# Softmax attention with fp32 queries and keys, fp32 scores in two row halves, and a new share of the split between VectorE and GpSimd

## The reference

```python
q = shape(hidden_states @ w_q)            # 16 heads of 64
k = shape(hidden_states @ w_k)
v = shape(hidden_states @ w_v)
scores = jnp.einsum('bhqd,bhkd->bhqk', q, k)
scores = scores + position_bias           # by head and distance
attn = jax.nn.softmax(scores.astype(jnp.float32), axis=-1).astype(scores.dtype)
ctx = jnp.einsum('bhqk,bhkd->bhqd', attn, v)
ctx = jnp.transpose(ctx, (0, 2, 1, 3)).reshape(B, S, INNER)
return ctx @ w_o
```

## Time and profile before

| | us |
|---|---|
| median of 3 runs | 2856.32 |
| lowest, highest | 2848.78, 2875.38 |
| span of the profiled execution | 2683.3 |
| softmax attention in it: first scores | 1426.6 |
| VectorE, ScalarE busy over the whole span | 2185.8, 1708.2 |
| TensorE, GpSimd busy over the whole span | 2000.1, 1788.5 |

### The profile page before, as it was taken

How to read it: one execution, slowest core, us unless ns; L and a number is a source line. 1 busy time by engine, 2 the same in 40 slices (tenths; PEclk the granted TensorE clock), 3 DMA queues, 4 the chain that set the end, 5 groups by cost and what they waited for, 6 DMA issues and landing times. The chain is left out here.

```text
span 2683.3 us, 62873 instructions
## 1 busy us (share of the span) xinstructions
PE 2000.1 (75%) x15627; PEld 1459.9 (54%) x15627; DVE 2185.8 (81%) x8149; ACT 1708.2 (64%) x4680; POOL 1788.5 (67%) x2414
## 2 busy tenths in 40 slices
PE   2329997485336999128887999999999999995887
PEld 2219887364226988115563555555555555553565
DVE  5427999686434999588999999999999999997897
ACT  3215554453224555145557999999999999995564
POOL 5765777102774777435645888888888888885555
PEclk9999999797558999559998999999999999998999
DMA  5134443402124444430003765666566656663000
GB/s 182 53 81 121 130 129 106 133 8 102 53 72 109 129 127 129 147 109 1 0 0 79 135 138 134 138 138 140 131 140 139 140 134 137 138 137 80 16 20 28
DMA packets 703411, 272.39 MB, mean 102 GB/s; under 512 B 560020, under 2 KB 688852, under 8 KB 702468
## 3 DMA queue, kind: packets, MB, share of 16 engines
q1 hardware_dynamic: 680628, 229.75, 35.0%
q0 software_dynamic: 17408, 35.82, 4.2%
q10 hardware_dynamic: 5200, 4.84, 0.6%
HBM read 59.31 MB, written 44.24 MB: 39 GB/s over the span
## 5 line engine op out<-in xcount | busy, mean ns | idle before, releaser
L2219 ACT ACTIVATE p_prob<-p_neg,p_neg_max 128x256 f32<-128x256 f32 x1024 | 509.0, 502 | 6.0 <-DVE p_neg_max L2111 5.8
L1044 POOL DMA_INDIRECT results_by_token<-p_e_result,p_e_slot x288 | 283.8, 985 | 156.9 <-DVE p_e_result L987 80.4
L2111 DVE CUSTOM_DVE_ANT_0 p_neg<-p_s_ps,top_bias 128x256 f32<-128x256 f32 x1024 | 380.5, 406 | 0.0
L2313 POOL TENSOR_TENSOR p_parts<-p_prob,p_parts 128x512 f16<-128x512 f32 x320 | 368.3, 1159 | 0.0
L2306 POOL TENSOR_SCALAR p_prob<-p_prob,p_inverse 128x256 f32<-128x256 f32 x640 | 328.8, 526 | 35.3 <-DVE p_inverse L2117 35.2
L730 POOL DMA_INDIRECT rows_by_expert<-p_r_z,p_r_target x256 | 247.5, 967 | 125.6 <-issue 105.3
L2346 PE MATMUL p_o_ps<-p_probT,p_val 128*128 128x256 f16 x1024 | 282.5, 276 | 62.0 <-DMA p_probT<-p_parts 61.6
L881 PE MATMUL p_e_o_ps<-p_w,p_e_hT 128*128 x2304 | 281.3, 276 | 0.2
L2347 PE MATMUL p_o_ps<-p_probT,p_val 128*128 128x256 f16 x1024 | 279.2, 273 | 0.0
L2348 PE MATMUL p_o_ps<-p_probT,p_val 128*128 128x256 f16 x1024 | 279.2, 273 | 0.0
L881 PEld LDWEIGHTS p_e_o_ps<-p_w,p_e_hT 128*128 128x128 f32 x2304 | 268.4, 192 | 3.5 <-issue 1.8
(11 more groups left out here) (282 smaller groups left out, 5609.2 us busy)
## 6 DMA issues: line engine op xcount, KB each, us to landing
p_e_z<-rows_by_expert SPq DMA_DIRECT2D x144, 129.0 KB
p_e_affine<-p_affine SPq DMA_DIRECT2D x144, 128.0 KB, 2.0
p_got<-results_by_token SPq DMA_DIRECT2D x64, 256.0 KB, 2.9
p_e_b<-p_b SPq DMA_DIRECT2D x144, 64.0 KB
p_probT<-p_parts SPq DMA_TRANSPOSE x512, 2.8
results_by_token<-p_e_result,p_e_slot POOLq DMA_INDIRECT x288
p_r_w<-in_w SPq DMA_DIRECT2D x2, 2048.0 KB, 10.1
p_w<-in_w SPq DMA_DIRECT2D x2, 2048.0 KB, 12.5
```

What stands on the lines that cost most here:

```text
L1044: pool.indirect_dma_start(dram_results, bass.IndirectOffsetOnAxis(ap=slot[q][:, t:t + 1], axis=0), result[q % 2][:, t, :], None).then_inc( ...
L2111: ins = v.tensor_tensor_reduce(neg[k % NEGS][:, t, :], s_ps[k % SCORES][:, t, :], bias[:, t, h, :], -1.0 / SCORE_SCALE, HUGE, ALU.add, ALU ...
L2219: ins = act.activation(prob[k % PROBS][:, t, :], neg[k % NEGS][:, t, :], ACT.Exp, bias=neg_max[k % NEGS][:, t:t + 1], scale=-1.0, accum_ou ...
L2313: pool.tensor_tensor(parts[k % PROBS][:, LOW, :, :], prob[k % PROBS][:], parts[k % PROBS][:, HIGH, :, :], ALU.subtract)\
```

## The change

1. Queries and keys are kept once, in fp32, instead of in two fp16 parts. ScalarE copies the bank and frees it; VectorE's low parts of queries and keys are gone. The scale of scores and bias becomes one.
2. Scores are fp32 matmuls: for each of two row tiles one in each row half, so 4 for a pair of units in the code in place of 12.
3. `SPLIT_BY` goes from three units of eight by VectorE (0, 2, 4) to five (0, 1, 3, 5, 6).
4. The projection slots of a quad alternate: query and key of the first pair, a pair of value tiles, query and key of the second pair, the other pair of value tiles. Value tiles still get two parts.
5. Semaphore counts follow. At the end, the last units' extra steps are only done where GpSimd splits the unit.

```diff
-FIRST_BANK = ((Q, 0), (Q, 1), (V, 0), (V, 2))
-SECOND_BANK = ((K, 0), (K, 1), (V, 1), (V, 3))
+FIRST_BANK = ((Q, 0), (V, 0), (Q, 1), (V, 2))
+SECOND_BANK = ((K, 0), (V, 1), (K, 1), (V, 3))
+PAIR_SLOTS = (0, 2)
+VALUE_SLOTS = (1, 3)
...
-SPLIT_BY = (BY_VECTOR, BY_POOL, BY_VECTOR, BY_POOL, BY_VECTOR, BY_POOL, BY_POOL, BY_POOL)
+SPLIT_BY = (BY_VECTOR, BY_VECTOR, BY_POOL, BY_VECTOR, BY_POOL, BY_VECTOR, BY_VECTOR, BY_POOL)
...
-        qkT = [m.sb(f"qkT{b}", [P, 2, 2, QUAD_PAIRS, GN], F16) for b in range(2)]
+        qkT = [m.sb(f"qkT{b}", [P, 2, QUAD_PAIRS, GN]) for b in range(2)]
...
-                    if has_slot(g, j // 2, ahead):
-                        (keep_low_second if j % 2 else keep_low_first)(*projection(i, g, j // 2))
+                    if j // 2 in VALUE_SLOTS:
+                        (keep_low_second if j % 2 else keep_low_first)(i, g, j // 2)
...
-            for n in range(QUAD_PAIRS):
-                keep_low_first(0, 0, n)
-                keep_low_second(0, 0, n)
             for k in range(3):
                 biased_max(0, k)
...
-            def take_high_first(i, g, n):
+            def take_first(i, g, n):
                 act.wait_ge(act_done, first_number(i, g, n))
-                high, scale = kept(g, HIGH, FIRST_BANK[n])
-                act.activation(high, act_ps[:], ACT.Copy, scale=scale).then_inc(high_ready, 1)
...
+                of, at = FIRST_BANK[n]
+                if of == V:
+                    act.activation(value(g, HIGH, at), act_ps[:], ACT.Copy, scale=VALUE_SCALE / (Z_SCALE * B_SCALE)).then_inc(high_ready, 1)
+                else:
+                    act.activation(qkT[g % 2][:, of, at, :], act_ps[:], ACT.Copy, scale=1.0 / (Z_SCALE * A_SCALE)).then_inc(act_taken, 1)
...
                 for k in range(1, GROUP_UNITS, 2):
-                    normalise(i, k)
+                    (high_part if split_by(k) == BY_VECTOR else normalise)(i, k)
...
-                passes = ((HIGH, HIGH), (HIGH, LOW), (LOW, HIGH))
                 for t in range(SEQ_TILES):
                     rows = slice(b * SEQ + t * P, b * SEQ + (t + 1) * P)
-                    for n, (q_part, k_part) in enumerate(passes):
-                        for h in range(2):
-                            half = slice(h * D_HEAD, (h + 1) * D_HEAD)
-                            ins = pe.matmul(s_ps[(k + h) % SCORES][:, t, :], qkT[g % 2][half, q_part, Q, pair, rows],
-                                            qkT[g % 2][half, k_part, K, pair, toks], start=n == 0, stop=n + 1 == len(passes))
...
+                    for h in range(2):
+                        half = slice(h * D_HEAD, (h + 1) * D_HEAD)
+                        ins = pe.matmul(s_ps[(k + h) % SCORES][:, t, :], qkT[g % 2][half, Q, pair, rows], qkT[g % 2][half, K, pair, toks],
+                                        start=True, stop=True)
...
-                    pe.wait_ge(act_taken, first_number(i, g, 2 + b))
-                    pe.wait_ge(v_taken, second_number(i, g, 2 + b))
+                    pe.wait_ge(act_taken, first_number(i, g, VALUE_SLOTS[b]))
+                    pe.wait_ge(v_taken, second_number(i, g, VALUE_SLOTS[b]))
```

More of the change, by code:

```diff
@@ L1736 @@
 A_SCALE = 2.0 ** 4
-QK_SCALE = 2.0 ** 5
 B_SCALE = 2.0 ** 4
@@ L1964, in g_use, with unmade @@
[L1964 to L1970, removed]
         def first_group(i):
             return isinstance(i, int) and i == 0
-        def second_use(i, g, n):
-            return i * (QUADS * GT) + (QUAD_PAIRS + g * GT + n - unmade(i, g))
+        def unmade(i, g, n):
+            return sum(slot <= n for slot in PAIR_SLOTS) if last_group(i) and g == QUADS - 1 else 0
@@ L2126, in keep_low_second @@
             def keep_low_second(i, g, n):
[L2127 to L2129 removed]
+                v.wait_ge(v_high, second_high_number(i, g, n))
+                tile = SECOND_BANK[n][1]
+                v.scalar_tensor_tensor(value(g, LOW, tile), v_ps[:], VALUE_SCALE / (Z_SCALE * B_SCALE), value(g, HIGH, tile),
+                                       ALU.mult, ALU.subtract).then_inc(v_taken, 1)
             def keep_low_z(i):
[L2132 removed]
+                v.wait_ge(high_ready, high_z_number(i))
                 v.scalar_tensor_tensor(zT[:, 1, :], act_ps[:], Z_SCALE, zT[:, 0, :], ALU.mult, ALU.subtract)\
@@ L2136, in keep_low_first @@
             def keep_low_first(i, g, n):
-                v.wait_ge(high_ready, first_number(i, g, n))
-                (high, scale), (low, _) = (kept(g, part, FIRST_BANK[n]) for part in (HIGH, LOW))
-                v.scalar_tensor_tensor(low, act_ps[:], scale, high, ALU.mult, ALU.subtract).then_inc(act_taken, 1)
+                v.wait_ge(high_ready, high_number(i, g, n))
+                tile = FIRST_BANK[n][1]
+                v.scalar_tensor_tensor(value(g, LOW, tile), act_ps[:], VALUE_SCALE / (Z_SCALE * B_SCALE), value(g, HIGH, tile),
+                                       ALU.mult, ALU.subtract).then_inc(act_taken, 1)
             def add_output(i, b):
@@ L2271, in _ @@
             take_high_z(0)
-            for n in range(QUAD_PAIRS):
-                take_high_first(0, 0, n)
-                take_high_second(0, 0, n)
+            for n in PAIR_SLOTS:
+                take_first(0, 0, n)
+                take_second(0, 0, n)
             exponent(0, 0)
@@ L2282, in _ @@
             for k in range(GROUP_UNITS - 2, GROUP_UNITS):
-                high_part(last, k)
+                if split_by(k) == BY_POOL:
+                    high_part(last, k)
             for b in range(GROUP_SEQS):
@@ L2444, in _ @@
                 ins.then_inc(b_done, 1)
-            turn_z(0, 0)
+            turn_z(0)
             pe.wait_ge(qk_low, 2)
-            for n in range(QUAD_PAIRS):
+            for n in PAIR_SLOTS:
                 project_first(0, 0, n)
```

91 lines of the change are left out of this document (52 added, 39 removed).

## The result

The changed kernel takes 2880.96 us (median of 9 runs, 2872.01 to 2893.74) against 2852.56 us for the kernel before on the same chip (9 runs): 1.0103 times as long, interval 1.0076 to 1.0129, +28.4 us. (A ratio is taken over all runs, not from the two medians.) The prediction was about 2884 us, +28. A second comparison gave 1.0101 (1.0068 to 1.0133), +32.4 us.

A forecast was written before the change was run, and what follows sets the result against it. VectorE, with ScalarE nearly full, was taken to set the pace: 65.3 - 63.4 = 1.9 us a group, times 16 groups, less 2 at the ends, +28; 2856.3 + 28 = about 2884 us, range 2815 to 2920.

The forecast's parts named there:

- the walk: Step-by-step timing of one round of eight units on VectorE and GpSimd; four rounds plus 1.9 us gave 64.7 to 66.7 us.
- the lower half: VectorE's period taken as 65.3 of 64.7 to 66.7 us, since a VectorE held up by TensorE meets fewer subtractions.
- slots 1, 2 and 6: VectorE's unit steps in a round of eight where GpSimd's subtraction holds low_part, ending at 3.45, 6.6 and 13.1 or 14.0 us.
- TensorE's scores +0.31 us a pair: Fp32 scores: four steps a half, 0.87 us against 0.66, plus 0.11 weight load; row halves side by side; 5.0 us a group.
- TensorE's need 62.9: TensorE's time a group in us: 56.5 before, 61.5 with fp32 scores, 62.9 with the wait for z.
- ScalarE about 56, GpSimd 47.9: Needs in us a group after ScalarE loses 8 high parts and GpSimd trades normalise and subtract for high_part; neither bounds.
- The ends, -2 us: Attention stage: 1 us saved at the start by fewer low parts, 1 us at the last unit's subtraction.
- What lies around it, 173 us up to the median: Time between the profiled execution's span, 2683.3 us, and the median, 2856.3 us; claimed untouched by the change.
- (c): Rival: a pair's score matmuls start in written order, a fifth step of 0.22 us; TensorE 66.4 us, +46 us; chance 0.07.
- (d): Rival: score row halves run in turn; TensorE 14 us a group more, 77 us, +220 us; chance 0.03.
- (a): Rival: TensorE paces and subtractions slip past low_part; 61.5 to 64.2 us a group, -32 to +11 us; chance 0.25.
- The rival on the faster side: Rival: VectorE not held, loses its waits, weight load hides; 60.4 to 61.7 us a group, -50 to -29 us; chance 0.20.

The follow-up runs named there:

- e_short_sub: Changed kernel with GpSimd's subtraction done on 32 of 256 columns of each row tile, the rest left zero; 0.9970 of the kernel before, period 63.0 us.
- e_two_pass: Changed kernel with two of three passes of the output product, the values' low part left out; 1.0083 of the kernel before, period 64.7 us.
- e_split_four: Changed kernel with VectorE splitting units 0, 2, 4 and 6 of eight; 0.9965 of the kernel before, period 63.0 us.

## Why the prediction was right, point by point

- **The pace is VectorE's, 65.3 us a group.** Right; measured 65.1 to 65.8, 65.3 in the middle. e_short_sub and e_two_pass show it from both sides. That it came out to a tenth is luck: the walk gave 64.7 to 66.7 us of work without waits, and there are 63.3 of work and 2.0 of waits for ScalarE's value copies, which no step of the walk had. The reason given for the lower half, a VectorE that TensorE now and then holds up, is not what happened: no wait of VectorE for TensorE shows. "No idle of VectorE" was said only of the low parts of queries and keys, but the value lines took the wait over. Slots were a little shorter than walked (slot 1, 2.52 us against 2.70, slot 4, 1.72 against 1.95), which paid for it.
- **`low_part` is held by the subtraction in slots 1, 2 and 6.** Right in place and size: over eight groups held ones are those of units 0, 1 and 5 only, which are these slots. Mean 752 ns ("above 750"), 2.7 in ten over 1.1 us ("two or three in ten"). The rule of the Trainium skill that the prediction weighed ("SBUF — State Buffer", "Who interferes with whom") agrees with it, and e_short_sub with both: a `low_part` that takes 0.47 us took up to 1.54, so 1.07 us longer, less than one subtraction of 1.16.
- **TensorE's scores +0.31 us a pair, halves side by side.** Right in sum, 1.37 against 1.08. The 0.31 us before the first score stayed what it was in the earlier trace rows; the whole difference lies from the first score to the output, 1.06 against 0.77. The 0.11 that the prediction put before the first score, for a weight load, lies between the first and the second start of each half (0.32 in place of 0.22).
- **TensorE's need 62.9.** It was not on trial in the changed kernel but was in e_split_four and e_short_sub: 63.0. This was partly luck. The work came out as 61.5, but the wait for z is 0.8 us and not 1.4, and 0.7 us at the scores, for the key copied behind the four rows of z, was missing.
- **ScalarE about 56, GpSimd 47.9.** 57.7 and 49.8 busy. GpSimd's instructions also lengthen beside VectorE's: the subtraction 1.20 us on average over these groups, 1.14 in the walk. Both have room, so it cost nothing.
- **The ends, -2 us.** Wrong in sign. The start of the stage gained some 0.6 us of the 1 forecast: from the first transposing of z to the second it took 43.1 us before and 43.55 after, where 17 units at the new period would have added 1.0. The end did not: from the last transposing of z to the last output the trace of before has 101.6 us and that of after 107.4. At the new period 48 units' worth of that, 1.5 groups, would be +2.9; another 2.9 is a longer end. Why it is longer was not followed. By stage the change costs 33.3 us in one trace and 31.6 in the other; the medians said 28.4 and 32.4 in two jobs. That the first median's difference is the +28 of the prediction is luck too.
- **"What lies around it, 173 us up to the median".** Wrong in what it is. The span of after's profile is within 2 us of its own run's time, so nothing of that size lies around a span. The profiled execution of before must come from a job where the rest of the program was faster: its span of 2683.3 is the level of two later jobs, in which the kernel before took 2682.69 and 2683.74 us. It cancelled, since it stood on both sides of the sum.
- **The rivals.** (c) and (d) are excluded by the step of 1.37 us; they would have made it 1.6 and 2.3. (a), that the subtractions slip past, did not happen: GpSimd waited for inverses 124 us in eight groups and so stayed in step with VectorE. The rival on the faster side needed both no holding and a cheap weight load; e_short_sub shows that no holding alone gives 63.0 and 0.3 % less time, not its 60.4 to 61.7.

## What to carry to other kernels

Two engines that look equally busy are told apart by shortening the work of each in turn, and both; VectorE's busy time here fell from 63 to 54 us by an edit on another engine. When work is moved between two engines that hold each other, find the best split by steps of one unit: here three of eight was even, four was better by 0.35 % and five worse by 1 %. And an edit that frees an engine is worth what the next bound leaves: read that one's stalls in the freed kernel and take them away there, because the same edit in the old kernel may be a loss.

## What the runs showed of the hardware

- A VectorE `low_part` (128x256, fp16 from fp32) takes 0.47 us alone, at most 0.70 beside GpSimd's 128x256 multiplications and up to 1.54 us beside its 128x512 subtraction; the subtraction in turn takes 1.16 us in 72 of 96 cases in the changed kernel and 1.31 in 23. Reducing it to 32 of 256 columns freed VectorE of 9.4 us of busy time a group.
- In the row halves, four fp32 matmuls of 256 columns each (two records a matmul) took 1.06 us to the next output, against 1.76 for eight records in series at the 0.22 us of the earlier trace rows.
- The stages outside the attention took about 1650 us in some jobs and 1800 or more in others, with the same program and the same granted clock in the attention (1.00 in the earlier trace rows and in the changed kernel's group). Most of it is in the two mixtures of experts: their first transposing of rows (L858) started at 200.9 and the last at 1071.0 us in the profile of before, at 238.6 and 1245.5 in that of after: 137 us of the 175 lie between them. In slices 4 to 6 of 40 the profile's page of after shows 115, 103 and 104 GB/s, that of before 121, 130 and 129. Two jobs on one chip differed in this way too; what sets it stays open, and a ratio within a job doesn't see it.
